# A gated delta-rule layer on one core: decay exponents from broadcast rows instead of TensorE products

## The reference

```
mixed = silu(causal_conv4(x @ W_qkv.T));  q, k, v = split(mixed);  z = x @ W_z.T
g  = cumsum over the chunk of -exp(A_log) * softplus(a + dt_bias);  beta = sigmoid(b)
decay[i, j] = exp(g[i] - g[j])  for j <= i, else 0
A  = -(k_beta @ k.T * decay), strictly lower;   Tm = (I - A)^-1
u = Tm @ v_beta;  kcd = Tm @ (k_beta * exp(g))
for each chunk:  v_new = u - kcd @ S;  out = (q*exp(g)) @ S + (q @ k.T * decay) @ v_new
                 S = S * exp(g_last) + (k * exp(g_last - g)).T @ v_new
out = out * rsqrt(mean(out^2) + 1e-6) * norm_w * silu(z) @ W_out.T, summed over heads
```

## Time and profile before

| | |
|---|---|
| median of 3 runs | 4606.46 us (4604.29 to 4607.61) |
| profiled execution, span | 4601.9 us |
| TensorE busy | 4346.1 us, 94% |
| VectorE busy | 3834.6 us, 83% |
| ScalarE busy | 2846.0 us, 62% |
| GpSimd busy | 2695.4 us, 59% |
| DMA | 209.77 MB, mean 46 GB/s |

### The profile page before, as it was taken

One profiled execution on the slowest core, in us unless ns is written; L12 is line 12 of the kernel. 1 busy time (PEld: TensorE's weight loads), 2 busy tenths in 40 slices (PEclk: granted clock), 3 DMA queues, 4 the chain that ended last, 5 costly groups with the idle time before them and its releaser, 6 DMA issues. The chain is left out here.

```text
span 4601.9 us, 94001 instructions
## 1 busy us (share of the span) xinstructions
PE 4346.1 (94%) x31188; PEld 3239.7 (70%) x31188; DVE 3834.6 (83%) x8326; ACT 2846.0 (62%) x5356; POOL 2695.4 (59%) x8592
## 2 busy tenths in 40 slices
PE   4799999999999999999999999999999999998798
PEld 2477777777777777777777777777777777776444
DVE  6688988889888898888988889888888888985554
ACT  3466666666666666666666666666666666664111
POOL 1566666666666666666666666666666666664000
PEclk7899999999999999999999999999999999999899
DMA  3212212122121221212121221222222122120200
GB/s 106 45 41 48 49 35 48 41 48 50 34 59 39 50 48 34 50 48 50 36 58 42 47 48 39 45 50 48 48 47 46 42 47 49 38 44 20 70 14 19
DMA packets 575837, 209.77 MB, mean 46 GB/s; under 512 B 455180, under 2 KB 539660, under 8 KB 574328
## 3 DMA queue, kind: packets, MB, share of 16 engines
q1 hardware_dynamic: 574392, 200.48, 19.4%
q0 software_dynamic: 960, 3.28, 0.3%
HBM read 155.84 MB, written 47.81 MB: 44 GB/s over the span
## 5 line engine op out<-in xcount | busy, mean ns | idle before, releaser
L740 DVE SCALAR_TENSOR_TENSOR CV<-pp,CW,CV 128x1023 f32<-128x1023 f32 (+2 forms) x768 | 980.5, 1277 | 41.4 <-ACT CV L1122 24.5
L343 PE MATMUL pp<-A,W 128*128 128x512 f32 x2048 | 963.7, 599 | 14.9 <-DVE CV L740 9.3
L1414 POOL TENSOR_TENSOR UL<-UL,TM 128x126 f32<-128x126 f32 (+22 forms) x1984 | 735.1, 370 | 155.4
L1411 POOL TENSOR_TENSOR TM<-UL,XL 128x126 f32<-128x126 f32 (+22 forms) x1984 | 706.4, 356 | 148.3 <-issue 13.6
L343 PEld LDWEIGHTS pp<-A,W 128*128 128x128 f32 x2048 | 373.5, 193 | 312.8 <-issue 293.3
L1210 ACT ACTIVATE QE<-qa,TAB 128x128 f32<-128x128 f32 x1024 | 318.3, 362 | 425.6 <-PE qa L482 425.5
L863 DVE SCALAR_TENSOR_TENSOR St<-St,TAB,kv 128x128 f32<-128x128 f32 x1024 | 308.7, 343 | 234.9 <-PE kv L501 227.1
L1221 ACT ACTIVATE VS<-qa,EB 128x128 f32<-128x128 f32 x1024 | 319.2, 364 | 292.0 <-PE qa L492 286.0
L545 PE MATMUL emit<-Wo,NTr 128*128 128x256 f32 x2048 | 487.5, 381 | 1.1 <-ACT NTr L1255 1.1
L524 PE MATMUL emit<-Wz,A 128*128 128x256 f32 x2048 | 484.9, 380 | 1.6 <-DVE A L914 1.6
L900 DVE SCALAR_TENSOR_TENSOR CO<-CO,ty,SZ 128x128 f32<-128x128 f32 x1024 | 420.4, 469 | 64.3 <-POOL ty L1398 60.6
(11 more groups left out here) (232 smaller groups left out, 9463.4 us busy)
## 6 DMA issues: line engine op xcount, KB each, us to landing
W<-wqkv SPq DMA_DIRECT2D x256, 128.0 KB, 3.7
XL<-xb SPq DMA_DIRECT2D x128, 256.0 KB, 4.1
UL<-c_u SPq DMA_DIRECT2D x64, 256.0 KB, 2.9
xb<-X SPq DMA_DIRECT2D x512, 32.0 KB, 1.6
Wz<-wz SPq DMA_DIRECT2D x64, 256.0 KB, 2.7
ub<-UL SPq DMA_DIRECT2D x128, 128.0 KB, 2.9
N<-ub SPq DMA_DIRECT2D x256, 64.0 KB, 2.2
Wo<-wo SPq DMA_DIRECT2D x64, 256.0 KB, 3.8
```

The lines of the kernel that those rows point to most:

```text
L343: ins = t.matmul(bk.pp[:, 512 * h:512 * h + 512], m.W[:, c, k, :], m.xnT[:, w // KH % 2, c, 512 * h:512 * h + 512], start=c == 0, stop=c == 1)
L740: v.scalar_tensor_tensor(m.CV[:, t, d:S], bk.pp[:, 0:S - d], m.CW[:, w % KH, t, 3 - d:4 - d], m.CV[:, t, d:S], ALU.mult, ALU.add).then_inc ...
L1411: gp.tensor_tensor(m.TM[:, 0:a, 0:b], m.UL[:, 0:a, k:k + 1].to_broadcast([128, a, b]), m.XL[:, k, k + 1:32].unsqueeze(1).to_broadcast([128 ...
L1414: gp.tensor_tensor(m.UL[:, 0:a, k + 1:32], m.UL[:, 0:a, k + 1:32], m.TM[:, 0:a, 0:b], ALU.subtract).then_inc(s["sub"], 1)
```

## The change

- TensorE's `decp` and VectorE's `mk` go, with the bf16 pieces, GL, GR and DEC. The users of `strip` are fewer.
- g as rows (128 rows of 1024: sequence and head by token) is stored once to DRAM. `ldg` loads the two rows of an item broadcast to all 128 partitions into GB (two buffers, 128 x 2 x 1024, 1 MB), and a small table AB with beta's logarithm minus g by token, which is the bias.
- `gm` on GpSimd adds the mask (0 or -1e30) to GB in place, two instructions of 128x1024 per item, behind the first `vsc`, for an item two later. For items 0 and 1, VectorE does it (`gmd`).
- `dec` is now 16 instructions of 128x128 per item, four per group, exp(GB + AB) with AB as bias per partition, in place.
- On ScalarE, the second group (`dec(u + 1, 1)`) now stands ahead of the second `sz`, and the third group (`dec(u + 1, 2)`) behind the third `sz`.
- In the start, `pj(0, 2, .)`, `kred(0)` and `nk(0)` move behind the barrier, SyncE issues the first broadcast load ahead of it, and `dec(0, .)` runs in ScalarE's `tables()`. The ring of GpSimd's DMAs is set to 8192 bytes.

```diff
@@ main_sp ldg
-        sp.wait_ge(s["decp"], 4 * w)
-        for r in range(2):
-            q.dma_start(m.GR[3 * r:3 * r + 3, r, :], dr.gcd[2 * kh + r, :, t0:t0 + S]).then_inc(s["dg"], 16)
-        q.dma_start(m.GL[6:12], dr.gad[2 * kh:2 * kh + 2, :, t0:t0 + S].rearrange("h q t -> (h q) t")).then_inc(s["dg"], 16)
+        kh, b = w % KH, w // KH
+        sp.wait_ge(s["g3a"], 16)
+        if w > 1:
+            sp.wait_ge(s["strip"], STRIP["kq", w - 2, 3] + 1)
+        q.dma_start(m.GB[w % 2][:].rearrange("p r c t -> p r (c t)"),
+                    dr.gcd[32 * b + 2 * kh:32 * b + 2 * kh + 2, :].unsqueeze(0).to_broadcast([128, 2, S])).then_inc(s["dg"], 16)
+        if w:
+            sp.wait_ge(s["tabw"], 80)
+            sp.wait_ge(s["dec"], 4 * (w - 1))
+            q.dma_start(m.AB[w % 2][:], dr.abd[kh, :, b * CH:(b + 1) * CH, :]).then_inc(s["dg"], 16)
@@ main_pe
-    def decp(w, q):
...
-            ins = t.matmul(bk.strip[:, c * 256:(c + 1) * 256], m.GL[:, cc], m.GR[:, :, cc], start=True, stop=True)
-        ins.then_inc(s["decp"], 1)
@@ main_dve
-    def mk(w, q):
...
-        v.tensor_tensor(m.DEC[n % 2][:], by(bk.strip[:], 4), g.mask.unsqueeze(1).to_broadcast([128, 4, 128]),
-                        ALU.min).then_inc(s["strip"], 1)
+    def gmd(w, r):
...
+        v.tensor_tensor(m.GB[w % 2][:, r], m.GB[w % 2][:, r], g.mask.unsqueeze(1).to_broadcast([128, CH, 128]),
+                        ALU.add).then_inc(s["gmd"], 1)
@@ x and att
-                                         m.RHO[w % 2][:, 2 * q + c:2 * q + c + 1], m.DEC[n % 2][:, 2 * c:2 * c + 2, :],
+                                         m.RHO[w % 2][:, 2 * q + c:2 * q + c + 1], m.GB[w % 2][:, :, 2 * q + c, :],
@@ main_act dec
-        ac.wait_ge(s["strip"], STRIP["dec", w, q] + 1)
-        a.activation(m.DEC[n % 2][:], m.DEC[n % 2][:], ACT.Exp).then_inc(s["dec"], 1)
+        if w < 2:
+            ac.wait_ge(s["gmd"], 2 * w + 2)
+        else:
+            ac.wait_ge(s["gm"], 2 * (w - 1))
+        for c in range(2):
+            for r in range(2):
+                row = m.GB[w % 2][:, r, 2 * q + c, :]
+                ins = a.activation(row, row, ACT.Exp, bias=m.AB[w % 2][:, 2 * q + c, r:r + 1])
+        ins.then_inc(s["dec"], 1)
@@ main_act loop
+            dec(u + 1, 1)
             sz(u - 1, 1)
-            dec(u + 1, 1)
...
+            sz(u - 1, 2)
             dec(u + 1, 2)
-            sz(u - 1, 2)
@@ main_pool
+    def gm(w, r):
...
+        po.wait_ge(s["dg"], 16 + 32 * w)
+        gp.tensor_tensor(m.GB[w % 2][:, r], m.GB[w % 2][:, r], g.mask.unsqueeze(1).to_broadcast([128, CH, 128]),
+                        ALU.add).then_inc(s["gm"], 1)
@@ main_pool loop
             vsc(u + 1, 0)
+            gm(u + 3, 0)
+            gm(u + 3, 1)
             tv(u, 2)
@@ main_dve start: the five splits of p.ra and of p.rb
-            v.tensor_copy(pc[:, 0, :], row).then_inc(s["pieces"], 1)
...
```

More of the change, by code:

```diff
@@ L269, in start @@
             q.dma_start(dr.xnd[b], p.xnT[b]).then_inc(s["xnw"], 16)
[L270 to L273, removed]
+        sp.wait_ge(s["gst"], 5)
+        q.dma_start(dr.gcd, p.ra).then_inc(s["g3a"], 16)
+        ldg(0)
+        for sem, n in (("cb", 16), ("lcl", 16), ("nws", 1), ("xnw", 32)):
             sp.wait_ge(s[sem], n)
-        ldg(0)
     def loop():
@@ L374, in tpq @@
         ins.then_inc(s["tpq"], 1)
-    def decp(w, q):
-        if not inside(w):
-            return
-        pe.wait_ge(s["strip"], STRIP["dec", w, q])
-        pe.wait_ge(s["dg"], 48 * (w + 1))
-        for c in range(2):
-            cc = slice((2 * q + c) * 128, (2 * q + c + 1) * 128)
-            ins = t.matmul(bk.strip[:, c * 256:(c + 1) * 256], m.GL[:, cc], m.GR[:, :, cc], start=True, stop=True)
-        ins.then_inc(s["decp"], 1)
     def kq(w, q):
@@ L585, in start @@
             tpk(0, h)
-        for h in range(2):
-            pj(0, 2, h)
     def tables():
@@ L1309, in tables @@
                          ACT.Exp).then_inc(s["egt"], 1)
+        for i in range(4):
+            dec(0, i)
         a.activation(tab(p, EGLB), cols(p.DL), ACT.Exp).then_inc(s["egt"], 1)
@@ L1431, in ng @@
                         ALU.mult).then_inc(s["EB"], 1)
+    def gm(w, r):
+        if not inside(w):
+            return
+        po.wait_ge(s["dg"], 16 + 32 * w)
+        gp.tensor_tensor(m.GB[w % 2][:, r], m.GB[w % 2][:, r], g.mask.unsqueeze(1).to_broadcast([128, CH, 128]),
+                        ALU.add).then_inc(s["gm"], 1)
     def vsc(w, h):
@@ L1477, in start @@
         gp.memset(m.N1[1][:], 0.0)
-        nk(0)
-        for k, d in enumerate((dr.gcd, dr.gad)):
-            po.wait_ge(s["pieces"], 5 * k + 5)
-            for b in range(1, NB):
-                gp.dma_start(d[:, :, b * S:b * S + S], p.pieces[k][32 * b:32 * b + 32]).then_inc(s["g3w"], 16)
     def tables():
         po.wait_ge(s["egt"], 4)
-        po.wait_ge(s["dtab"], 1)
+        po.wait_ge(s["dtab"], 2)
         for k in range(4):
@@ L1531, in loop @@
         vsc(0, 0)
+        gm(2, 0)
+        gm(2, 1)
         nk(1)
@@ L1887, in program @@
             p.ra, p.rb, p.rc, p.rd = (m.QK[:, i, :] for i in (1, 2, 4, 5))
-            p.pieces = [m.X[1][:].rearrange("p u d -> p (u d)"), m.V[1][:].rearrange("p c r d -> p (c r d)")]
-            p.pieces = [t[:, 0:1536].bitcast(BF16).rearrange("p (k t) -> p k t", k=3) for t in p.pieces]
             p.GC, p.BT = (m.K[i][:].rearrange("p c (t h) -> p (c t) h", h=32) for i in (1, 2))
@@ L1940, in consts @@
     f[:, 128] = 1.0
-    mask = np.where(j > q, -1e30, 1e30).astype(np.float32)
-    gr = np.zeros((12, 2, S // 2), np.int32)
-    gr[6:9, 0] = gr[9:12, 1] = 0x3F803F80
+    mask = np.where(j > q, -1e30, 0.0).astype(np.float32)
     u0 = np.zeros((2, 64, 16, 32), np.float32)
@@ L1948, in consts @@
     reset[:, ::128] = 0.0
-    return f, mask, gr, reset, u0.reshape(128, 16, 32)
+    return f, mask, reset, u0.reshape(128, 16, 32)
 def kernel(**inputs):
@@ L1972 @@
     wi = np.concatenate(gu + [dt], 1).reshape(128, KH, WC).transpose(1, 0, 2)
-    cf, mask, gr, reset, u0 = consts()
+    cf, mask, reset, u0 = consts()
     arrays = {
```

133 lines of the change are left out of this document (48 added, 85 removed), and 2 rows, old and new, of the table SEMS.

## The result

The changed kernel takes 5403.4 us (median of 4 runs, 5388.4 to 5414.9), the kernel before 4605.4 in the same comparison: a ratio of 1.1735, 95% interval 1.1712 to 1.1758. The direction is the forecast's, the size is not: 5403 lies 143 us above the 5260 forecast and 73 above the end of the range. The profiled execution of after has a span of 5407.7 us.

The account below looks back on a forecast made before the run. TensorE, busy in 94% of the span, bounds the kernel. Terms of 3.4 + 3.8 + 1.1 + 2.7 = 11.0 us a turn over 62 turns add 682 us; 4606 + 682 - 28 = 5260 us, range 4860 to 5330.

Parts of the forecast that it names:

- second place: GpSimd's mask additions meet VectorE's second normalisation group at the shared port, so TensorE's CO transposes come 3.4 us a turn later.
- first place: ScalarE's third exponentials, now behind the third silu of z, delay X, CO and TensorE's transposes by 3.8 us a turn.
- clock: TensorE runs below full clock after its two new waits each turn: 2.7 us a turn, bounds 0 and 3.4.
- exponent products: Four products a turn leave TensorE, which wins at most 1.3 us a turn.
- one way or the other: One normalisation first or both GpSimd additions first: either way the second normalisation group ends about 3.6 us later.
- Third meeting: The third normalisation group falls beside GpSimd's second V scaling and one weight addition: 1.1 us a turn.
- Start: TensorE's wait at the barrier between start and loop mostly goes: -28 us, bounds -45 and +5.
- Costed at nothing: The 1 MB broadcast load, AB's small load and the wider additions in waits were given no cost.
- Rival 4: Both places cost, but no clock is lost: 5093 us, chance 22%.
- Rival 2: Only the port costs, as X isn't held by the exponentials: 4938 us, chance 6%.
- Rival 1: Only ScalarE's order costs; VectorE's normalisations pass between GpSimd instructions without loss: 4815 to 4920 us, chance 17%.
- X's idle: Sign in the profile after: VectorE's X idles some 4 us for ScalarE's exponentials; small idle would refute the ScalarE order cost.

Follow-up runs that it names:

- e17: The changed kernel with idle matmuls in both of TensorE's long waits, 5 and 4 of 128x512: 5127.2 us.
- e13: The changed kernel with 5 idle matmuls of 128x512 in TensorE's first long wait only: 5231.9 us.
- e14: The changed kernel with 4 idle matmuls of 128x512 in TensorE's second long wait only: 5234.4 us.
- e4: The changed kernel with each GpSimd mask addition cut into four pieces of 128x256 at the same place: 5107.7 us.
- e1: The changed kernel with the third group of exponentials put back ahead of the third silu of z on ScalarE: 5051.1 us.
- e2: The changed kernel with both mask additions moved behind the second V scaling and held for the third normalisation: 5007.9 us.
- e3: The changed kernel with third exponentials back ahead of the third silu, and both mask additions behind the second V scaling, held for the third normalisation: 4662.3 us.
- e12: The kernel before with four additions of 128x512 of no use on GpSimd behind the first V scaling: 4855.3 us.

## Why the forecast came out as it did

By its terms, in us a turn:

| step | forecast | measured | from |
|---|---|---|---|
| second place: port, wait of the CO transposes | 3.4 | 4.3 | (309.8 - 41.9)/62 |
| first place: order on ScalarE | 3.8 | 3.6 | 224.2/62 |
| third group meets the second V scaling | 1.1 | 0 | 1.13 us for four |
| clock | 2.7 | 5.5 | e17; e13 + e14 |
| KS waits for the state | none | 0.7 | 42.6/62 |
| exponent products | in the first two | -1.4 | see below |
| sum | 11.0 | 12.7 | a turn: 13.1 |

- **First place: right**, mechanism and size. Undone it gave 352 us (5.7 a turn, wait and clock), and alone in the kernel before it cost 440. Only the customer was wrong: QS, not the transposes.
- **Second place: right mechanism, price a little low.** The addition was priced by the V scaling's row, 1.89 us; with its operands it takes 2.38, two of them 1.0 more, and that is the 0.9 missing. What I left at "one way or the other" is settled by e4: one instruction each, by turns.
- **Third meeting: wrong in the changed kernel.** The slow turn and the first place hold the group back until the scaling is done. I added costs that exclude each other; in e1 and e17, where one is taken away, it appears (2.77 and 1.79 us for four).
- **Clock: the step that failed.** Its size, 2.7, and its upper bound, 3.4, came from one stretch of before, 4195 to 4200, at 0.66: 1.7 us lost behind a wait of 4.3, taken twice. The row was read rightly (the clock is 1.00 again from 4199 on); that every wait of the loop costs what this one did was the error. The loop shows 5.5, twice the forecast and beyond the bound, with waits of 4.9 and 3.6, the one a little longer than that one, the other shorter. I had made the loss a function of the wait in front of it. The rows of one turn say otherwise: 9 us at half speed behind 3.6, 5 us behind 4.9. What does set it stays open. (5.5 - 2.7) x 62 = 174 us is more than the whole miss.
- **The products: 1.3 us was about right, but not kept.** At full clock, in a turn of e17 beside the one of before, the four steps that held a product are shorter by 0.22, 0.56, 0.22 and 0.45 us, 1.45 in all. Where the second product stood, KS of chunk 6 now waits for the state (0.63 us a turn in the rows; before, 6 us in the whole span). And the forecast took only some 0.4 off its two places.
- **Start: -17, not -28.** The barrier's 16 us are gone as forecast (the table's first transposes at 64.33 instead of 83.72). The 12 us more are not: TensorE waits 12.17 us at 97.58 for the first convolution on VectorE. In VectorE's queue it stands behind a weight comparison, which waits for GpSimd's cast at 92.80, and that stands behind GpSimd's stores of the tables, the last two at 90.50 and 91.65.
- **Costed at nothing:** the broadcast load and AB. The table of waits has one of 9.5 us on GpSimd and one of 1.1 on VectorE for them, both before the loop (starts at 148.8 and 110.72; the first memset is at 161.6), and none after. That holds.

The rows of the start in the changed kernel (TensorE, VectorE, GpSimd):

```profile
97.58 2.90 PE L339 MATMUL pp<-A,W 128*128 128x512 f32 x3 [12.17 <-DVE CV L714]
...
93.25 0.36 DVE L896 TENSOR_SCALAR wd<-ix,lc 128x268 f32<-128x268 f32 x1 [9.96 <-POOL ix L1429]
93.53 3.91 DVE L714 SCALAR_TENSOR_TENSOR CV<-pp,CW,CV 128x1023 f32<-128x1023 f32 x3
...
90.50 1.16 POOL L1450 DMA_DIRECT2D tabd<-V  x1 [7.27 <-issue]
91.65 1.15 POOL L1452 DMA_DIRECT2D abd<-V  x1
92.80 0.42 POOL L1429 CAST ix<-ix 128x268 f32<-128x268 int32 x1
```

Against the forecast: clock +174, port +56, KS +43, start +11; the meeting -68, products -87, order -12. That is +117, where 143 are to be explained; the 0.4 us a turn that the table's sum leaves unplaced, 25 us, are the rest, and with the clock at 5.8 or 5.9, as the other two ways have it, hardly any of it would be unplaced. Rival 4, both places without the clock, stood at 5093, and e17, the changed kernel at full clock, took 5127: without the clock the forecast was 34 us out, in part because port, KS and products cancel. Rival 2, the port alone, stood at 4938; e1 took 5051, the rival's price being low for port and clock both. Rival 1, the order alone, stood at 4815 to 4920; e2 took 5008, the price being low by the clock. Of what was to show it, X's idle (5.55 us, 4 forecast) and the slow normalisations (up to 2.48 us, 1.9 forecast) came larger, the turn too (77.1, 75 forecast). The prediction gives the forecast's own range once as 5180 to 5310 and once as 5080 to 5320; 5403 lies outside both.

## What to carry to other kernels

Price a new wait of TensorE by both parts, the time it stands and what it does slowly after it, and take the second from several stretches, not from one: here it was some 5.5 us for 8 us of waits, and filling the waits with idle matmuls measured it directly. On GpSimd ask of each new elementwise instruction which VectorE instructions with two SBUF inputs, or comparisons like the one in e3, are due meanwhile: hold it on their semaphore or cut it in pieces, since VectorE gets one in between each. Before adding up two costs, check whether the first delays the victim of the second past it.

## What the runs showed of the hardware

- VectorE's normalisations and GpSimd's additions alternated, one instruction each, whether an addition was long or short: four normalisations took 5.31 us beside two additions of 2.38, 4.33 beside additions of 1.1 (e12), and 3.04 beside pieces of 0.7.
- The weight comparison, with one tensor input (128x268), took 2.12 us instead of 0.35 beside a mask addition.
- An addition of 128x1024 with a mask broadcast along chunks takes 2.34 to 2.44 us on GpSimd, a multiplication of the same size by a value broadcast along rows 1.89.
- In one turn TensorE stayed at 1.2 GHz for over 9 us of uninterrupted work behind a wait of 3.6 us. With 4.3 and 3.4 us of idle matmuls in the waits of 4.9 and 3.6 (e17) the granted clock was 1.00 in the stretches read behind both, 0.988 over the span.
